# Four feed-forward pair steps woven between the last images, and three changes of order inside a pair step

## What is computed

```python
h = concat(cls_tok, patches(x) @ W + b)          # 64 x 197 x 192
h = h + attention(layernorm(h))                  # 12 heads of 64, 4-bit fake quantisation
h = h + ffn(layernorm(h))
# ffn, on each row of 192:
def bitlinear(x, w, g):                          # w ternary
    x = rmsnorm(x, g)                            # x * rsqrt(mean(x*x) + 1e-6) * g
    s = 127 / max(max(abs(x)), 1e-5)             # one factor per row
    return (round(x * s) / s) @ w_q.T
up, gate = split(bitlinear(x, w_in, g_in), 2)    # 192 -> 2 x 512
out = bitlinear(silu(gate) * up, w_out, g_out)   # 512 -> 192
```

## Time and profile before

| what | value |
|---|---|
| median of 3 runs | 1281.3 us (1279.3 to 1283.15) |
| profiled execution, its own time | 1279.7 us |
| its span, first to last instruction | 1277.7 us |
| mean granted TensorE clock | 0.893 |
| busy share PE / DVE / ACT / POOL | 86% / 85% / 73% / 36% |
| image stage | about 225 to 912 us |
| feed-forward stage | 915.8 to 1277.7 us |

### The profile page before, as it was taken

The page is one execution under the profiler, slowest core; times in us unless marked ns, Lnnn a source line. Parts: engine busy times, 40 slices in busy tenths (PEclk is TensorE's granted clock), DMA queues, the critical chain, the costliest instruction groups (busy, mean ns, idle before and its releaser), DMA issues.

```text
span 1277.7 us, 31970 instructions
## 1 busy us (share of the span) xinstructions
PE 1098.7 (86%) x10782; PEld 678.1 (53%) x10782; DVE 1086.9 (85%) x1979; ACT 933.1 (73%) x1877; POOL 462.4 (36%) x540
## 2 busy tenths in 40 slices
PE   7999995799999999999999999996367577777776
PEld 6999995245555555555555555554233344444443
DVE  6666777189999999999999999999479989899886
ACT  0000000699999999999999999995178888888886
POOL 5544434002211222211112221112256666666664
PEclk9999998699999999999999999998566867777776
DMA  8999994136655655555555665555212322223222
GB/s 284 313 282 294 292 308 161 44 129 161 160 144 142 141 147 159 159 145 141 145 147 160 152 146 142 148 147 143 52 53 82 93 82 84 86 82 90 86 75 73
DMA packets 158358, 187.63 MB, mean 147 GB/s; under 512 B 42864, under 2 KB 119744, under 8 KB 158016
## 3 DMA queue, kind: packets, MB, share of 16 engines
q1 hardware_dynamic: 90656, 138.99, 34.3%
q10 hardware_dynamic: 52224, 37.37, 9.5%
q0 software_dynamic: 15360, 9.70, 8.0%
HBM read 143.06 MB, written 36.12 MB: 140 GB/s over the span
## 4 chain that ended last, share of the span: by engine, by line
PE 71%; ACT 9%; issue 7%; DVE 6%; DMA 3%; POOL 2%; ACTq 1%; SPq 0%; DVEq 0%; POOLq 0%
PE psum L1066 13%; PE psum L1131 12%; PE psum L1194 11%; PE psum L1164 7%; PE psum L1134 7%; PE psum L1227 6%; PE psum L1147 6%; PE psum L1181 5%; ACT yi L608 2%; ACT big L601 2%; ACT ysq L628 2%; DVE big L1041 1%; PE psum L1248 1%; ACT zi L616 1%; PE psum L1082 1%
## 5 line engine op out<-in xcount | busy, mean ns | idle before, releaser
L917 DVE TENSOR_TENSOR pi<-big 128x2364 int16<-128x2364 f32 (+1 forms) x128 | 333.2, 2603 | 11.4 <-DMA big<-z_row 11.3
L707 POOL DMA_DIRECT2D h_res<-att x128 | 135.3, 1153 | 563.7 <-ACT att L545 554.5
L569 ACT ACTIVATE big<-psum 128x788 f32<-128x788 f32 (+1 forms) x384 | 330.3, 862 | 0.4 <-DVE pi L917 0.3
L531 ACT ACTIVATE qki<-psum 128x394 int16<-128x394 f32 x384 | 172.5, 509 | 17.4 <-PE psum L1134 5.6
L1066 PE MATMUL psum<-big 128*128 128x192 f32 (+1 forms) x1128 | 182.5, 326 | 1.5 <-DMA big<-xt 1.5
L1066 PEld LDWEIGHTS psum<-big 128*128 128x128 f32 (+1 forms) x1128 | 180.6, 188 | 2.6 <-issue 1.8
L1227 PE MATMUL psum<-winb,zT 96*128 96x512 bf16 (+1 forms) x396 | 146.9, 538 | 31.1 <-DVE big L1041 30.2
L1194 PE MATMUL psum<-big,sa_hot 128*32 128x197 f32 (+1 forms) x3072 | 168.9, 337 | 0.6 <-DVE zt L941 0.6
L531 ACT ACT_TABLE_LOAD x1 | 1.3, 1283 | 226.6 <-PE psum L1134 226.6
L741 POOL TENSOR_TENSOR big<-big,goutb 128x512 f32<-128x512 f32 (+1 forms) x99 | 123.8, 1271 | 80.3 <-DVE big L1041 80.3
L1131 PE MATMUL psum<-xT,w1b 128*128 128x394 bf16 x384 | 108.3, 342 | 25.2 <-DMA xT<-x_int 16.2
(11 more groups left out here) (105 smaller groups left out, 1826.2 us busy)
## 6 DMA issues: line engine op xcount, KB each, us to landing
big<-z_row SPq DMA_DIRECT2D x192, 394.0 KB, 5.0
big<-xt SPq DMA_DIRECT2D x98, 384.0 KB, 4.6
tin<-h_res SPq DMA_DIRECT2D x49, 192.0 KB, 2.4
tres<-h_res ACTq DMA_DIRECT2D x49, 192.0 KB, 2.5
out<-oo ACTq DMA_DIRECT2D x49, 192.0 KB, 2.6
h_res<-big ACTq DMA_DIRECT2D x78, 96.0 KB, 4.4
h_res<-att POOLq DMA_DIRECT2D x64, 96.0 KB, 3.1
x_int<-big ACTq DMA_DIRECT2D x93, 64.0 KB, 4.2
```

What stands on the lines that cost most here:

```text
L531: act.activation(qki[:, k, :, :], psum[:, bank, 0:2 * N] .rearrange("p (c n) -> p c n", c=2), ACT.Copy, scale=factor[(F_Q, F_K)[b % 2]])\
L569: act.activation(ex[0:r, tri, t, 4 * g:4 * g + 4, :].rearrange("p (a h) n -> p a h n", a=2), psum[0:r, 2 * t:2 * t + 2, 0:2 * N] .rearrang ...
L707: pool.dma_start(h_res[bass.ds(b - 4, 1), t0:t0 + r, :].rearrange("a n d -> (a n) d"), att[0:r, par, t, :], accum_op=ALU.add).then_inc(s_a ...
L917: v.tensor_tensor(pi[0:r, t, :, 0:N], ex[0:r, it, t, :, :], zb[0:r, ip, :, :], ALU.mult).then_inc(s_pi, 1)
```

## The change

- Four steps `pair_step(0)` to `pair_step(3)` (`EARLY = 4`) are taken out of the loop over pairs and placed between the last image steps, at another place on each engine. With B = 64: DVE runs step 0 inside image step 65, steps 1 and 2 after image step 66, step 3 after 67; ACT and PE run steps 0 and 1 after image step 66, 2 and 3 after 67, then image step 68; POOL runs 0 and 1 after image step 65, 2 and 3 after 66, then 67.
- The waits for all images are gone. A load of pair t waits for the images that it reads (`wait_added`), written out for the steps outside the hardware loop. SP loads `tin` one step ahead: in step t that of pair t+1.
- PE does both groups of transposes before the hidden matmuls.
- DVE aggregates (L1021) before the maximum of |yg|, and takes the maximum of |zc| last in the step.
- The dequantisation factors get a tile of their own, `ft`, with four copies. DVE writes them between the reciprocal and the last product, ahead of `y`, and the wait for `y` before them is gone.
- The two copies that fill `wdeq4` come before the images on DVE. The hardware loop starts at t = 14 instead of 10.

```diff
-        MS, RMS, MAX, T_, A127, INV, S_, F_ = range(8)
+        ft = sb("ft", [128, 4, 2, 2], fp32)
+        MS, RMS, MAX, T_, A127, INV, S_ = range(7)
...
-            first = (LAGS + 3) // 2 * 2
-            for t in range(first):
-                step(t, t % 2)
+            first = 14
+            for t in range(EARLY, first):
+                step(t, t % 2, t % 4)
...
+        EARLY = 4
+
+        def images(image_step, first, last):
+
+            for b in range(first, last + 1):
+                image_step(b, b % 2, b % 3)
+
+        def pairs(pair_step, first, last):
+
+            for t in range(first, last + 1):
+                pair_step(t, t % 2, t % 4)
+
+        def wait_added(eng, t):
+
+            last = (256 * (t + 1) - 1) // N if t < 8 else B - 1
+            for p in range(2):
+                wait(eng, s_added[p], 32 * ((last - p) // 2 + 1))
...
@block.sync
-            for p in range(2):
-                sp.wait_ge(s_added[p], 32 * (B // 2))
-
-            def pair_step(t, par):
-                if at := pair_of(t)(0):
-                    r, n = at
-                    wait_apart(sp, s_t["zc"], t - 1)
-                    sp.dma_start(tin[0:r, par, 0:n, :], pair_rows(h_att, t, r, n)).then_inc(s_t3[par], 16)
+            def pair_step(t, par, q):
+                pair, oth = pair_of(t), 1 - par
+                if at := pair(-1):
+                    r, n = at
+                    if isinstance(t, int):
+                        wait_added(sp, t + 1)
+                    wait_apart(sp, s_t["zc"], t)
+                    sp.dma_start(tin[0:r, oth, 0:n, :], pair_rows(h_att, t + 1, r, n)).then_inc(s_t3[oth], 16)
+
+            images(image_step, -2, B + 4)
+            wait_added(sp, 0)
+            sp.dma_start(tin[:, 0, :, :], pair_rows(h_att, 0, 128, 2)).then_inc(s_t3[0], 16)
+            pairs(pair_step, 0, EARLY - 1)
             over_pairs(sp, pair_step)
...
@block.scalar
-            for p in range(2):
-                act.wait_ge(s_added[p], 32 * (B // 2))
+            images(image_step, -2, B + 2)
+            pairs(pair_step, 0, 1)
+            images(image_step, B + 3, B + 3)
+            pairs(pair_step, 2, EARLY - 1)
+            images(image_step, B + 4, B + 4)
             over_pairs(act, pair_step)
...
                 if at := pair(4):
                     r, n = at
+                    if isinstance(t, int):
+                        wait_added(act, t - 4)
                     act.dma_start(tres[0:r, par, 0:n, :], pair_rows(h_att, t - 4, r, n)).then_inc(s_t3b[par], 16)
...
@block.gpsimd
+            images(image_step, -2, B + 1)
+            pairs(pair_step, 0, 1)
+            images(image_step, B + 2, B + 2)
+            pairs(pair_step, 2, EARLY - 1)
+            images(image_step, B + 3, B + 3)
             over_pairs(pool, pair_step)
...
@block.vector
-                        v.tensor_tensor(V(F_), V(A127), wdeq4[:, :, :], ALU.mult).then_inc(s_t["dequant"], 1)
+                        v.tensor_tensor(ft[:, q, :, :], V(A127), wdeq4[:, :, :], ALU.mult).then_inc(s_t["dequant"], 1)
...
                 factors(2)
-                if at := pair(0):
-                    r, n = at
-                    dve.wait_ge(s_t["zc"], t + 1)
-                    v.tensor_reduce(val(0, par, MAX, r, n), zc[0:r, par, 0:n, :], AX.X, ALU.max,
-                                    apply_absolute_value=True).then_inc(s_t["amax"], 1)
+                factors(4)
                 factors(3)
...
-                if at := pair(3):
-                    dve.wait_ge(s_t["y"], 2 * (t - 3) + at[1])
-                factors(4)
...
                     ins.then_inc(s_t["o_ready"], 1)
+                if at := pair(0):
+                    r, n = at
+                    dve.wait_ge(s_t["zc"], t + 1)
+                    v.tensor_reduce(val(0, par, MAX, r, n), zc[0:r, par, 0:n, :], AX.X, ALU.max,
+                                    apply_absolute_value=True).then_inc(s_t["amax"], 1)
...
+                if b == B + 1:
+                    pairs(pair_step, 0, 0)
                 if has_unit(b, -2 * U1):
                     normalise(b - 2, par, (tri + 1) % 3, 0)
...
+            images(image_step, -2, B + 2)
+            pairs(pair_step, 1, 2)
+            images(image_step, B + 3, B + 3)
+            pairs(pair_step, 3, EARLY - 1)
             over_pairs(dve, pair_step)
...
@block.tensor
-            pe.wait_ge(evac["y"], B)
-            def pair_step(t, par):
+            def pair_step(t, par, q):
                 pair, oth = pair_of(t), 1 - par
+                if at := pair(2):
...
+                    pe.wait_ge(s_t["xi"], t - 1)
...
+                if at := pair(5):
...
+                    pe.wait_ge(s_t["yi"], t - 4)
...
                 if at := pair(3):
                     r, n = at
                     pe.wait_ge(s_t["xT_read"], t - 2)
...
+            images(image_step, -2, B + 2)
+            pairs(pair_step, 0, 1)
+            images(image_step, B + 3, B + 3)
+            pairs(pair_step, 2, EARLY - 1)
+            images(image_step, B + 4, B + 4)
             over_pairs(pe, pair_step)
```

More of the change, by code:

```diff
@@ L284, in vit_tower_kernel @@
         ORD = [0, 2, 1, 3]
-        def images():
-            return [(-1, 1), (0, 0)], [(B - 1, (B - 1) % 2), (B, B % 2)]
         U1 = 6
@@ L346, in over_pairs @@
                 for j in range(UNROLL):
-                    step(UNROLL * i + first + j, j % 2)
+                    step(UNROLL * i + first + j, j % 2, (first + j) % 4)
             for t in range(first + whole, NPAIR + LAGS):
-                step(t, t % 2)
+                step(t, t % 2, t % 4)
         def pair_rows(dram, j, rows, n):
@@ L357, in loads_of @@
             return 16 * ((j - par) // 2 + 1) if isinstance(j, int) else 8 * (j - par) + 16
-        def over_images(eng, step):
-            for b in range(-2, B + 5):
-                step(b, b % 2, b % 3)
+        EARLY = 4
[9 more added lines that the diff above has]
+                wait(eng, s_added[p], 32 * ((last - p) // 2 + 1))
         def dst_rows(dram, y, x, half, along_x):
@@ L601, in pair_step @@
                         act.activation(silu[0:r, a, :], psum[0:r, 2 * a + 1, :], ACT.Silu,
-                                       scale=pt[0:r, oth, F_, 0, a:a + 1]).then_inc(s_t["silu"], 1)
+                                       scale=ft[0:r, (q + 2) % 4, 0, a:a + 1]).then_inc(s_t["silu"], 1)
                 if at := pair(4):
@@ L1211, in image_step, with pair_step @@
                         scores(b, par, u)
-            over_images(pe, image_step)
-            pe.wait_ge(evac["y"], B)
-            def pair_step(t, par):
+            def pair_step(t, par, q):
                 pair, oth = pair_of(t), 1 - par
-                if at := pair(3):
-                    r, n = at
-                    pe.wait_ge(s_t["xT_read"], t - 2)
-                    for a in range(n):
-                        wait(pe, s_t["y"], 2 * (t - 4) + a + 1)
-                        for half in (1, 0):
-                            for c in range(2):
-                                last = mm(psum[0:r, 2 * a + half, :], zT3[:, oth, a, c, 0:r],
-                                          winb[:, c, half * HID:(half + 1) * HID],
-                                          start=(c == 0), stop=(c == 1))
-                        last.then_inc(s_t["hid"], 1)
                 if at := pair(2):
@@ L1250, in pair_step @@
                     last.then_inc(s_t["yT_summed"], 1)
+                if at := pair(3):
+                    r, n = at
+                    pe.wait_ge(s_t["xT_read"], t - 2)
+                    for a in range(n):
+                        wait(pe, s_t["y"], 2 * (t - 4) + a + 1)
+                        for half in (1, 0):
+                            for c in range(2):
+                                last = mm(psum[0:r, 2 * a + half, :], zT3[:, oth, a, c, 0:r],
+                                          winb[:, c, half * HID:(half + 1) * HID],
+                                          start=(c == 0), stop=(c == 1))
+                        last.then_inc(s_t["hid"], 1)
                 if at := pair(5):
```

168 lines of the change are left out of this document (82 added, 86 removed).

## The result

The kernel with the change takes **1266.2 us** (median of 4 runs, 1265.4 to 1268.7) against 1280.4 (1279.3 to 1283.2) for the one before on the same chip: a ratio of 0.989, 95% interval 0.987 to 0.991, so 14.1 us less. The forecast was 1271.5 in a range of 1256 to 1281, against 1281.3 before. It is faster, as foreseen, by 14.1 us where 9.8 were foreseen.

A forecast was written before the change was run, and what follows sets the result against it. No engine was full: a loop between engines bounded the step, and DVE, ACT and PE idled at the hand-over. 1279.7 - 12.7 + 3.5 = 1270.5 for the profiled execution, 1.6 under the median; forecast 1271.5, range 1256 to 1281.

The forecast's parts named there:

- The hand-over: From the images to the first y of step 5: four early steps gain 12.7 us, between 9 and 16.
- the images' tail: Last image steps: pair 0's DVE step ahead of the last normalisation moves them 4.0 us later, 4.7 at most.
- From zi to the first y: Start of the pair steps: 8.95 us before, of which 2.4 was taken as the next DVE step.
- 8.8 us for step 4: Ramp: y of step 3 at 918, DVE's factors of step 4 at 926.8, behind the last image's transfer on POOL.
- The steady step: Steps 5 to 50: 6.93 us each instead of 6.86, +3 us over 45 steps.
- the low loop: Steady step at PE's low clock: zi, transposes, hidden matmuls, silu, yi and zi add up to 7.67 us.
- the fast steps: Steady step at PE's high clock: the loop sums to 5.37 us, but ACT alone needs 6.4.
- Rival B: Steady part: new loop hidden by a high clock, ACT bounds at 6.4 to 6.6 us, total 1252; chance 0.14.
- Rival C: Steady part: new loop bounds and the clock stays low, 7.67 us a step, total 1305; chance 0.11.
- Rival D: Between images and pairs: overlap doesn't come, some 3 us left of 12.7, total near 1281; chance 0.13.
- DVE's order: Steady step on DVE: frees 0.5 us, sum 5.6, factors 0.4 earlier; worth nothing since DVE bounds no step.
- The drain: End of the kernel, at the low clock: costs another 0.5 us.

The follow-up runs named there:

- the weave alone: Changed kernel with the old orders on PE and DVE, leaving the four early steps, loads a step ahead and the ring: 1267.9 us, 0.992 against the kernel before.
- the first run: Changed kernel with PE doing the hidden matmuls before both groups of transposes again, as before the change: 1265.2 us, 0.990 against the kernel before.

## Why the prediction was right, and where it was not

**The hand-over: mechanism right, 12.7 too small by 2.9 us.** It measured 15.6 us from image 60 on. Counted from `att` of image 60, zi of pair 0 came after 21.8 us where I had 23.0; y of step 3 came 6.5 us behind it where I had 7 (911 to 918); y of step 4 came 7.6 behind that where I had 8.8, queued behind the transfer as said; and y of step 5 followed after 6.1, as forecast. The first of these is mostly the images' tail, which moved by 3.1 us instead of 4.0: pair 0 started at 895.5 in an execution 1.6 us ahead, about a microsecond sooner than the 898.0 forecast.

**From zi to the first y the number was right by luck.** I took 8.95 us from the rows and subtracted 2.4 for the next DVE step, which makes 6.55; 6.48 came. But in the kernel before the first y didn't wait for that DVE step. It waited for the silu behind zT, and zT for x transposes that stood behind the hidden matmuls (928.65, 929.32 in the rows above), so the 2.4 were not to be taken off. What shortens this stretch is PE's order, which I had priced in the steady loop alone, and at nothing here. With the old order in the weave it is 9.4 us (the weave alone), or 7.5 where the hidden matmuls took 1.90 us instead of 3.6 (the first run). So the weave by itself was overpriced, 11.1 us for 12.7, and the transposes' order brought the 2.6 to 4.3 that I had not counted. (The zi at 923.00, which the prediction calls pair 1's, is pair 0's.)

**The clock in the ramp.** The 8.8 us for step 4 were worked out with rows of the low clock. In the kernel after, and in the run with pair 0's step moved, the first hidden matmuls took 1.89 us at a granted clock of 1.00 and the step 7.6. In the runs with DVE's old order and with SP's transfers they took 3.62 at 0.50, the step 8.8 and 8.6, and the hand-over 43.8 and 43.6. The clock alone doesn't settle the hand-over, though: with zi between the silus and SP's transfers together they took 1.89, and it was 43.4. No run varied the clock by itself.

**The steady step: the loop right, the mean in part luck.** 6.93 forecast, 6.92 measured; the low loop 7.67 forecast, 7.63 measured, and the fast steps 6.3 to 6.4 where the sum had 6.4. That this loop bounds is shown (9 us when zi leaves it). The mean was a choice between two ways for the clock, whole steps in turn (7.04) and a rise within each step (6.84). Neither came: 12 of 45 steps were low, and the mean is that of a first part of 7.10 and a second of 6.81. The extra 3 us against before are not beyond doubt: the traces with transposes first have 6.82 to 6.95 (mean 6.90 of six), those with hidden matmuls first 6.79 to 6.87 (6.84 of three). The difference of these means would cost 2.6 us, but the groups overlap.

**Rival B's size was out of reach for a reason that I did not see.** It took ACT's own work as the next bound. Behind zi's loop lies a wait for yi, then the chain over POOL, and only with three more edits to the step and no hardware loop did it reach B's 6.5. **Rival C** did not come: the mean clock of the steady part was 0.79. **Rival D** fell with the weave alone, 11.1 us of hand-over.

**DVE's order** was worth nothing in the total, as costed: the product took 0.13 us and DVE's sum fell to 254.35/45 = 5.65 (forecast 5.6). I had left out a possible meeting of the product with POOL's power in its new place. They do meet, in 27 of 45 steps, and the product still took 0.124 to 0.134 us in all 45. The rule on the shared port pair in the Trainium skill (SBUF — State Buffer, Who interferes with whom), that a VectorE instruction with two SBUF inputs contends with a GpSimd one that reads SBUF, agrees with the old place, where the product took 0.68 us beside yg and ended as the first yg did (1106.00 and 1105.97). In the new place this trace doesn't show the product blocked. If anything waited there, it was the power, and POOL's recorded times are rough.

**The drain and the sum.** The drain was put at +0.5 and is 0.7 shorter; it is 22.0 to 23.6 us long in the traces of this document, so that is within its scatter. The sum of the prediction, 1270.5 plus the 1.6 by which the profiled execution lay under the median, makes 1272.1; the 1271.5 that I wrote is 0.6 lower, without a reason. The image stage's scatter, 1.6 us in the profiled execution, is no part of the change.

**Open:** why the clock rose for the first hidden matmuls in some executions of the hand-over and not in others; and whether the orders on PE and DVE are worth 1 or 2 us of the total or nothing, since the weave alone at 1267.9, the old DVE order at 1266.4 and the changed kernel at 1266.2 lie within each other's intervals.

## What to carry to other kernels

An order that is priced in the steady loop has to be priced once more in the ramp, where the same waits are not hidden by work of other steps: here it was worth 2.6 to 4.3 us in the hand-over and cost about as much in 45 steps. When a sum takes a term out of a measured stretch, check in the timeline that the stretch waited for it. When no engine is full, write down the loop with its rows and take one link out; in this kernel the next one was a few tenths behind or less each time (6.92, 6.72, 6.66), so promise only the distance to it, and look for links in which nothing computes, as the hand-over to POOL in the hardware loop.

## What the runs showed of the hardware beyond what I had expected

- In this hardware loop the same step is slower than written out: 6.67 against 6.53 us within one trace, 6.62 against 6.51 over the 45 steps of two. The hand-over from ACT to POOL took 0.29 against 0.08 us. Over the 45 steps POOL idled 34 us for the squares' sum with the loop and 27 without. Whether the added `sem_inc`, the waits on register values or something else of the loop costs it was not tried.
- A VectorE product of 128x4 took 129 ns in one place and 563 (before: 0.68 us) in another, for the same operands. Beside GpSimd's yg, two instructions of 1.27 us, it was long; beside GpSimd's power of 0.7 to 0.9 us it was not.
- The eight hidden matmuls that open the ramp took 1.89 or 3.62 us in traces of kernels with the same order on PE, by the granted clock.
